# Issuing eight scatters of a half back to back after one wait, in a graph-propagation kernel on one core

## What is computed

```python
def _propagate(all_emb, rows, cols, vals):
    acc = all_emb
    x = all_emb
    for _ in range(N_LAYERS):                       # 3
        x = jax.ops.segment_sum(vals[:, None] * x[cols], rows, num_segments=N_NODES)
        acc = acc + x
    return acc / (N_LAYERS + 1)
...
users_emb = all_users[users] + _upsample_nearest(mm_users[users])
items_emb = all_items + _upsample_nearest(mm_items)
rating = users_emb @ items_emb.T
rating = rating + bias_user[users] + bias_item.T
return jax.nn.sigmoid(rating)
```

## Time and profile before

| | us |
|---|---|
| timed, median of 3 runs | 6020.74 (6016.39 to 6022.49) |
| span of the profiled execution | 6906.3 |
| sort, up to the first messages | 1430 |
| message stages of the three layers | 1311, 1170, 1166 |
| unit stages of the first two layers | 557, 557 |
| last unit stage and ratings | 715 |

### The profile page before, as it was taken

One profiled execution on the slowest core, in us unless ns is written; L12 is line 12 of the kernel. 1 busy time (PEld: TensorE's weight loads), 2 busy tenths in 40 slices (PEclk: granted clock), 3 DMA queues, 4 the chain that ended last, 5 costly groups with the idle time before them and its releaser, 6 DMA issues.

```text
span 6906.3 us, 175021 instructions
## 1 busy us (share of the span) xinstructions
PE 4000.4 (58%) x57424; PEld 3370.0 (49%) x57662; DVE 5194.9 (75%) x7652; ACT 4083.1 (59%) x10026; POOL 2327.8 (34%) x2074
## 2 busy tenths in 40 slices
PE   5300211056766766776566666677656666657777
PEld 4300111045665665665555555566555565556652
DVE  9999999965555555999655555599965555559997
ACT  0055565244444445999555555599955555559987
POOL 0044333034444444000455555500045555550000
PEclk9755555577777777999777778799978777779998
DMA  9500000044444444665444444466544434446669
GB/s 338 201 0 0 0 0 0 5 112 142 143 142 140 143 138 140 162 161 138 133 144 141 141 141 142 140 162 161 138 136 144 140 140 142 141 136 162 161 166 317
DMA packets 737418, 921.22 MB, mean 133 GB/s; under 512 B 68254, under 2 KB 585279, under 8 KB 736977
## 3 DMA queue, kind: packets, MB, share of 16 engines
q1 hardware_dynamic: 646112, 670.30, 34.5%
q0 software_dynamic: 90944, 249.26, 10.0%
q10 hardware_dynamic: 304, 1.00, 0.1%
HBM read 533.93 MB, written 386.43 MB: 133 GB/s over the span
## 4 chain that ended last, share of the span: by engine, by line
DVE 41%; issue 21%; PE 16%; another core or an unknown queue 13%; ACT 5%; DMA 2%; DVEq 2%; POOL 0%; SPq 0%; POOLq 0%; ACTq 0%
DVE ring L1235 9%; PE psum L1473 6%; DVE store L1028 5%; DVE ring L1192 4%; PE psum L1475 4%; DVE ring L1277 4%; PE psum L1511 3%; ACT ring L671 3%; DVE ring L1271 3%; DVE new L1286 3%; DVE store L1006 2%; DVE total L823 2%; DVE store L1007 2%; DVE ring L1268 1%
## 5 line engine op out<-in xcount | busy, mean ns | idle before, releaser
L737 POOL DMA_INDIRECT posts<-ring x1884 | 1908.0, 1013 | 3078.9 <-ACT ring L657 2614.5
L657 ACT ACTIVATE ring<-ring 128x64 f32<-128x64 f32 x7536 | 1885.0, 335 | 1782.3 <-DVE ring L1192 1109.9
L1473 PE MATMUL psum<-store,ring 128*128 x15072 | 2192.4, 261 | 1007.9 <-DVE ring L1235 584.7
L1473 PEld LDWEIGHTS psum<-store,ring 128*128 128x128 bf16 x15072 | 1801.7, 124 | 1175.8 <-issue 1148.7
L1192 DVE TENSOR_REDUCE ring<-psum 128x512 f32<-128x1024 f32 x942 | 1151.1, 1222 | 1513.7 <-remote 1468.5
L1475 PE MATMUL psum<-store,ring 128*128 x15072 | 2104.8, 229 | 150.2 <-issue 148.3
L1475 PEld LDWEIGHTS psum<-store,ring 128*128 128x128 bf16 x15072 | 1626.8, 115 | 226.4 <-issue 183.4
L1235 DVE TENSOR_SCALAR ring<-ring,lane_f 128x1024 bf16<-128x1024 bf16 x1884 | 843.3, 489 | 10.6 <-DMA ring<-lanes_d 10.6
L1505 PE MATMUL psum<-ring 128*128 128x64 bf16 x7584 | 562.4, 198 | 232.3 <-DVE ring L1271 228.5
L720 POOL TENSOR_TENSOR ring<-store 128x1024 f32<-128x1024 f32 x157 | 370.6, 2361 | 800.8 <-DVE store L1007 363.5
L1511 PE MATMUL psum<-ring 128*128 128x64 bf16 x15168 | 528.9, 194 | 151.9 <-DVE ring L1277 150.2
(11 more groups left out here) (232 smaller groups left out, 3970.6 us busy)
## 6 DMA issues: line engine op xcount, KB each, us to landing
ring<-lanes_d SPq DMA_DIRECT2D x471, 512.0 KB
ring<-posts SPq DMA_DIRECT2D x240, 516.0 KB
store<-posts SPq DMA_DIRECT2D x234, 516.0 KB
out<-new SPq DMA_DIRECT2D x96, 500.0 KB, 8.5
posts<-store SPq DMA_DIRECT2D x2, 20640.0 KB, 115.8
posts<-store SPq DMA_DIRECT2D x2, 20124.0 KB, 88.6
posts<-ring POOLq DMA_INDIRECT x1884
ring<-runs_d SPq DMA_DIRECT2D x78, 256.0 KB
```

The lines of the kernel that those rows point to most:

```text
L657: last = nc.scalar.activation(of, of, ACT.Copy, scale=vring[:, h, c * BLOCK + b:c * BLOCK + b + 1])
L737: pool.indirect_dma_start(out=posts[:, :], out_offset=bass.IndirectOffsetOnAxis(ap=dring[:, h, c:c + 1], axis=0), in_=msg[:, n, :], in_off ...
L1473: pe.matmul(psum[:, c, b * 2 * F:(b + 1) * 2 * F], of, xflat[:, bass.ds(at_d[c] * F + k * XT, 2 * F)], start=(k == 0), stop=False, skip_gr ...
```

## The change

GpSimd no longer waits before each scatter for that scatter's chunk. Ahead of the first scatter of a half it waits once, for the last chunk of the half (the eighth; in the rest, which has four chunks, the fourth), and then issues the scatters of the half without a wait between them. It is done so for both halves of each body and for the rest, in all three layers. All else is the same: the scatters, their order and their semaphores.

```diff
--- before.py
+++ after.py
@@ -732,7 +732,8 @@
                 def scatter(i, chunks):
                     for n in range(chunks):
                         h, c = n // 8, n % 8
-                        pool.wait_ge(s_msg, i * 16 + (done + n + 17))
+                        if c == 0:
+                            pool.wait_ge(s_msg, i * 16 + (done + min(n + 8, chunks) + 16))
                         pool.sem_inc(s_pace, 1)
                         pool.indirect_dma_start(
                             out=posts[:, :], out_offset=bass.IndirectOffsetOnAxis(ap=dring[:, h, c:c + 1], axis=0),
```

## The result

The changed kernel takes 6420.36 us (median of 4 runs, 6419.32 to 6424.80) against 6021.61 before: ratio 1.066, 95% interval 1.065 to 1.068, or 399 us more. The forecast was 6136, with 6240 as the upper end.

What follows compares the result with a forecast made beforehand. VectorE and TensorE were taken to bind the message stages, GpSimd beside the path. Refill stalls in layers two and three (+100 us) plus layer ends (+15) gave +115 us, 6136 us; own range 6060 to 6200, overall 6020 to 6240.

Steps and rivals of the forecast that it cites:

- What bounds the kernel: Message stages: bound by the loop of VectorE (join, hots) and TensorE (sums), with GpSimd, busy half of it, not binding.
- quick halves: Alternative bound: 82% of timed halves run at full clock, bound by GpSimd's 10.5 us, and go to 11.0: +63 us.
- The shorter timed execution: Message stages: all 886 us missing against the profiled execution come from their 3647, every half scaled by 0.757.
- The chain from last join to refill: Each half: scaling 2.05, latency to GpSimd 0.82, eight scatters 10.2, signal of their arrival 1.7; sum 14.8 us.
- the landing: After a half's last scatter, until its refill may run: taken as 1.7 us, between 0.5 and 2.16.
- the start: From the end of the eighth chunk's scaling to the first scatter on GpSimd: 0.82 us.
- The way back, refill to join: From a refill to the next half's last join: 9.05 us; two halves in 23.85 us, +0.64 each, +100 us.
- The first layer: Its halves: the same sum gives 11.9 to 12.1 us, below its 12.65, so no added time.
- The layer ends: SyncE's loads and the clearing at each layer's end come 4.9 us later; three layers, +15 us.
- A: Rival, chance 0.20: halves are long enough to hide the new wait; only layer ends cost, 6036 us (6020 to 6040).
- B: Rival, chance 0.13: TensorE's stalls lower its clock; a quarter more slow halves adds 141 us, 6277; all of them, 6600.
- C: Rival, chance 0.09: pairs run back to back after stalls, keeping TensorE's clock up; faster, 5888 us.

Runs made afterwards that it cites:

- second profile: The unchanged kernel profiled once more: 6014.95 us, with a span of 6013.2 us.

## Why the prediction was wrong, point by point

The loop that the forecast reckoned with is the one that the runs show. What failed are two terms of its sum: the chain from a half's last join to its refill, put at 14.8 us and measured at 17.8, and the half that it is set against, put at 11.27 and measured at 10.8.

**What bounds the kernel: wrong for the timed execution.** The step that called GpSimd "beside the path" rested on the earlier trace rows, where the clock was 0.75 and a half took 14.9 us. In the second profile the clock of layers two and three is 0.88 and 0.90, a half is 10.8 us, and GpSimd's 10.6 us are the bound; leaving out an eighth of its scatters gave 182 us. The text saw GpSimd's 10.5 us and used them as a bound for the "quick halves" only.

**The shorter timed execution: half right.** That the missing 886 us came out of the message stages is confirmed: 3647 us fell to 1052 + 866 + 858 = 2776, by 871. That they shrink alike was wrong: the first layer's half went to 13.3 us (12.65 assumed), the others' to 10.9 and 10.8 (11.27 assumed). The lower base is 0.4 to 0.5 us a half, some 70 us of the loss over 157 halves.

**The chain from last join to refill: right in its parts, mis-sized in two.** Over 74 halves of each of layers two and three the changed kernel has: scaling 2.05 (forecast 2.05); from there to the first scatter 1.7 (0.82); the burst 10.3 (10.2); issue end to refill 3.7 (1.7), or 3.6 where the refill did wait for it; together 17.8 us in place of 14.8. The first miss is the landing. It was read at a layer's end, where no load of lane numbers runs; inside the stage the hots that stand right before the refill release such a load, and it meets the last scatters. With small loads the landing fell to 2.5 and the start hardly (1.6), and 140 us came back, so that is shown; of the 130 us that holding the load back gave, a part is the earlier start. The second miss is the start: the bursts of the two halves can abut, so that one waits for the other; the forecast took the halves as evenly spaced. Where the load was held back, the halves were even and this start was 0.9 us, so the two go together; why they become uneven otherwise stays open.

Against the kernel before, it is the late start that costs. There join to refill took 13.2 us, with the first scatter 4.3 us ahead of the end of the scaling and 5.0 us from issue end to refill; the change puts the start 6.0 us later, and the landing gives 1.3 of it back.

**The way back, refill to join, and the loop of two halves: right.** 8.75 us were forecast, 8.05 measured. With them and 0.4 for the refill the forecast's own formula gives (17.8 + 0.4 + 8.05) / 2 = 13.1 us; 13.2 and 13.1 were measured. That this comes out is no test, since the two stretches make up two halves by definition; the tests of the loop are the scatter left out, which gave about half its time a half, and the one batched half, whose round set the body. So the formula was right, and the chain and the base put into it were not: 13.1 - 10.8 = 2.3 us for 157 halves is 360 us, where 0.64 had been put.

**The first layer: called free, costs 31 us in its halves.** Its half goes from 13.3 to 13.7. The chain there is 18.3 us with a landing of 5.1, not 14.8.

**The layer ends: right in the sum.** From a layer's last join to SyncE's first load 8.1, 8.3 and 10.2 us before and 14.9, 16.1 and 13.0 after: +17 us in all, 15 forecast, though 6.8, 7.8 and 2.8 in place of 4.9 each. The rest's four scatters stand behind the late burst, as reckoned from the earlier trace rows.

**The rivals.** A (the cover holds) is refuted, and its argument that GpSimd runs behind ScalarE had the wrong sign: that is just where standing still costs GpSimd. B (the clock falls) is not the cause: the granted clock of layers two and three does fall, from 0.88 and 0.90 to 0.82, but TensorE's part of the loop, from refill to join, is 8.05 us after and 7.8 to 7.9 before, 0.1 to 0.3 us more for two halves; so it bears about 0.1 us a half of the 2.3. C (the clock rises) is refuted: it did not rise. By the prediction's own test (a change of the clock by more than 0.05) B would have been called; that test was a bad one, since here the clock fell, with TensorE's busy share (0.70 to 0.59 in layer two), in stages whose loss it did not make.

**The sum.** Message stages +36, +182 and +181 us: from the first refill to the last they take 31, 178 and 183 us longer, and the ends 17, together 409; the two spans differ by 406 and the timed medians by 399.

## What to carry to other kernels

An engine that issues back to back in the stage that counts has no slack for a late start: bursts of four, which start 1.0 us later, cost 29 us here, and bursts of eight, 6.0 us later, 399. Look at its idle time before each instruction (here 0.30 us) rather than at its busy share of the span (39%). Where slots are recycled, write the round as a loop, from the last write of a slot to its release and back to the next last write, and size each term inside the stage where it runs: a landing read at a layer's end was too short here (1.7 us for 3.7). And a profile whose span is far from the timed median may have another bound: scaling it stage by stage hides that.

## What the runs showed of the hardware

A 132 KB scatter's landing depended on what else was being moved: from its issue's end to the refill that waits for it 3.7 us with a 512 KB load released just before, 2.8 with that load held back, 2.5 with loads of 64 KB (means of layers two and three). The Trainium skill (DMA: Bandwidth & Descriptors, Issuing engines are not separate DMA queues) says that transfers started by different engines run on the same DMA engines and interleave. The runs agree in that the load lengthens the landing, by 0.9 to 1.2 us. GpSimd took 0.96 us (1.00 to 1.04 in the mean) and 0.30 of gap for each indirect DMA of 128 rows whether it waited between them or not. Waiting for six chunks and then two kept nearly two thirds of the loss, and batching one half of two kept all of it: what stood behind the late burst on GpSimd's queue was late with it.
